# A fused decoder block on one core: the context turned by VectorE from square blocks, the sums behind the first adapter round, one wide rank-4 product

## What is computed

```python
x = x + attention(layernorm(x))            # scores = q k^T / 4, banded by sps_pro, softmax, times v, projection
x = x + gated(layernorm(x), ctx, ctx)      # 8 heads of 32; q k^T times exp(Dtilde - max), over a norm, then group norm
x = x + ffn(layernorm(x))                  # below

# gated: its gates see q, k and v, and k = v = ctx
itilde = einsum('bsd,hd->bhs', concat([q, ctx, ctx]), Wi_w) + Wi_b
ftilde = einsum('bsd,hd->bhs', concat([q, ctx, ctx]), Wf_w) + Wf_b
csum = cumsum(log_sigmoid(ftilde))

# ffn: tokens 1 to 16 of each sequence make low-rank adapters m1 (H x D) and m2 (D x H)
m1 = (even[:, :4, :, None] * odd[:, :4, None, :]).reshape(B, H, D)
m2 = (even[:, 4:, :, None] * odd[:, 4:, None, :]).reshape(B, D, H)
h = gelu(x W1^T + scale * x m1^T + b1)
out = h W2^T + scale * h m2^T + b2
```

## Time and profile before

| | us |
|---|---|
| median of the runs | 2023.12 |
| profiled execution, its own time | 2027.77 |
| its span, first to last instruction | 2026.0 |
| TensorE busy | 1940.2 (96%) |
| VectorE busy | 1522.6 (75%) |
| ScalarE busy | 1125.0 (56%) |
| GpSimd busy | 314.9 (16%) |

### The profile page before, as it was taken

The page is one execution under the profiler, slowest core; times in us unless marked ns, Lnnn a source line. Parts: engine busy times, 40 slices in busy tenths (PEclk is TensorE's granted clock), DMA queues, the critical chain, the costliest instruction groups (busy, mean ns, idle before and its releaser), DMA issues.

```text
span 2026.0 us, 47964 instructions
## 1 busy us (share of the span) xinstructions
PE 1940.2 (96%) x16404; PEld 1464.9 (72%) x16404; DVE 1522.6 (75%) x4318; ACT 1125.0 (56%) x2504; POOL 314.9 (16%) x257
## 2 busy tenths in 40 slices
PE   5789999999999999999999999999999999999988
PEld 4467777777777777777777777777777777777766
DVE  6577787778787778777778778777878777877742
ACT  2455566655556655556655556665555665555551
POOL 1111011111011111111111101111101111111110
PEclk9699999999999999999999999999999999999999
DMA  3000001110001111010110000011000111100000
GB/s 103 22 23 14 30 22 32 32 32 31 12 22 32 32 32 32 11 32 22 32 32 32 17 27 22 32 32 32 32 12 22 32 32 32 32 11 33 13 13 22
DMA packets 65583, 56.43 MB, mean 28 GB/s; under 512 B 13185, under 2 KB 65026, under 8 KB 65554
## 3 DMA queue, kind: packets, MB, share of 16 engines
q1 hardware_dynamic: 65554, 56.05, 8.9%
HBM read 37.15 MB, written 16.78 MB: 27 GB/s over the span
## 4 chain that ended last, share of the span: by engine, by line
PE 93%; DVE 4%; ACT 2%; issue 0%; DMA 0%; SPq 0%; DVEq 0%; ACTq 0%
PE UA L1290 16%; PE UB L1290 5%; PE TB L1232 5%; PE UB L1232 5%; PE UA L1232 5%; PE PV L1232 4%; PE UA L1240 3%; PE TA L1257 3%; PE TB L1372 3%; PE GT L1302 3%; PE TA L1372 3%; PE TA L1197 3%; PE TA L1101 3%; PE TB L1101 3%; PE QQ L1086 2%; PE UA L1310 2%
## 5 line engine op out<-in xcount | busy, mean ns | idle before, releaser
L1290 PE MATMUL UA<-W2f,hs_all 128*128 128x256 f32 x1536 | 349.1, 380 | 2.9 <-DVE ot L943 2.2
L1290 PEld LDWEIGHTS UA<-W2f,hs_all 128*128 128x128 f32 x1536 | 286.5, 190 | 62.3 <-issue 13.9
L957 DVE TENSOR_TENSOR C<-qT,QKs 128x512 f32<-128x512 f32 x256 | 169.3, 690 | 172.3 <-ACT qT L668 153.4
L550 POOL TENSOR_TENSOR Ng<-HT,gnw_b 128x256 f32<-128x256 f32 x128 | 94.9, 741 | 820.4 <-ACT HT L681 820.4
L531 POOL TENSOR_TENSOR xg<-x,gnb_b 128x1024 f32<-128x1024 f32 x32 | 75.9, 2372 | 811.1 <-DVE csum L893 811.1
L1290 PE MATMUL UB<-W2f,hs_all 128*128 128x256 f32 x512 | 115.8, 379 | 0.0
L659 ACT ACTIVATE hs_all<-UA,b1c 128x512 f32<-128x512 f32 x64 | 44.0, 687 | 109.6 <-PE TB L1240 109.6
L1290 PEld LDWEIGHTS UB<-W2f,hs_all 128*128 128x128 f32 x512 | 94.9, 190 | 11.7
L649 ACT ACTIVATE QKs<-TA 128x512 f32<-128x512 f32 x64 | 38.4, 600 | 108.9 <-PE DD L1257 108.9
L1257 PEld LDWEIGHTS TA<-xn2T,ctxT 32*128 32x128 f32 x512 | 63.2, 190 | 30.1 <-issue 27.7
L898 DVE TENSOR_SCALAR band_a<-sc 128x512 f32<-128x512 f32 x32 | 76.7, 2397 | 10.0 <-ACT sc L633 10.0
(11 more groups left out here) (311 smaller groups left out, 5532.3 us busy)
## 6 DMA issues: line engine op xcount, KB each, us to landing
xin<-x SPq DMA_DIRECT2D x32, 512.0 KB, 3.5
ctxn<-ctx SPq DMA_DIRECT2D x32, 512.0 KB, 3.8
out<-ot SPq DMA_DIRECT2D x32, 512.0 KB, 3.0
Ev<-xn SPq DMA_DIRECT2D x512, 1.0 KB
hs_all<-L_ffn_W SPq DMA_DIRECT2D x4, 512.0 KB, 8.7
T<-tok SPq DMA_DIRECT2D x128, 2.0 KB
moving<-parts SPq DMA_DIRECT2D x96, 8.0 KB, 1.9
QKs<-L_attn_W_qkv SPq DMA_DIRECT2D x1, 768.0 KB
```

What stands on the lines that cost most here:

```text
L550: pool.tensor_tensor(Ng[:, b, :].rearrange("p (k n) -> p k n", k=2), HT[:, b % 2, :, 0:P], gnw_b[:, :].rearrange("p (k n) -> p k n", k=2), ...
L957: dve.tensor_tensor(C[:, b % 2, 4 * hf:4 * hf + 4, :].rearrange("p h i -> p (h i)"), dx[hf], QKs[:, b, 4 * hf:4 * hf + 4, :].rearrange("p ...
L1290: ins = pe.matmul(OB[b][:, 0:D], hs_all[:, k, b * S:(b + 1) * S], W2f[:, k, :], start=(i == 0), stop=(i == KH - 1))
```

## The change

Three edits in each step.

1. The context is loaded twice. `ctxn` stays for `vc`. Beside it SyncE issues eight transfers, one for each 32 features, which put the context into `bands` (the two band buffers, now one tensor of 128 x 2 x 512) so that every 32 x 32 square lies where its turned copy is wanted. They wait for `y_ok` and come after the `Ev` rows and before the E rows. VectorE turns all squares in one instruction, behind `head_sums(1)` and ahead of `rinv`. `turn_ctx` and `evac_ctxT` are gone.
2. `sums` moves from behind `up(2)` to behind `up_adapter(0)`. GpSimd's `xg` waits for `xn3l` in place of `csum`.
3. `low_rank` makes all four sequences' products against all tokens in eight matmuls of 512 columns; `gT` adds the bias row and multiplies by `own_g`, which holds the scale for a token's own sequence and zero for the others.

```diff
+        bands = sb("bands", [P, 2, N])
+        band_a, band_b = (bands[:, i, :] for i in range(2))
+        ctx_blocks = bands[:, :, :].rearrange("p k (n c) -> p k n c", c=32)
...
+        c_blocks = ctx_in.rearrange("(g b) (i a) d -> g a (b i) d", b=G, a=32)
...
                 if SELF.on(it):
-                    sp.wait_ge(ctxT_mm.h, ctxT_mm.at(it, 0))
                     sp.wait_ge(vc_ok.h, vc_ok.at(it, 1))
                     sp.dma_start(ctxn[:, :, :], c_g[it]).then_inc(ctx_loaded.h, 16)
...
                 if FFN.on(it):
                     ev_rows(it)
+                if SELF.on(it):
+                    sp.wait_ge(y_ok.h, y_ok.at(it, 1))
+                    for h in range(HEADS):
+                        sp.dma_start(ctx_blocks[32 * (h % 4):32 * (h % 4) + 32, h // 4, :, :],
+                                     c_blocks[it][:, :, 32 * h:32 * h + 32]).then_inc(blocks_loaded.h, 16)
                 if CROSS.on(it):
                     e_rows(it)
...
-                    pool.wait_ge(csum_ok.h, csum_ok.at(it, 1))
+                    pool.wait_ge(xn3l_ok.h, xn3l_ok.at(it, 2))
                     pool.tensor_tensor(xg[:, :, :], x2[:, :, :], gnb_b[:, :].unsqueeze(1).broadcast_to([P, G, D]),
                                        ALU.add).then_inc(xg_ok.h, 1)
...
-            def evac_ctxT(it):
-                evac(it, ctxT_mm, ctxT_ok, [QQ, DD], ctxT, [qk_mm])
...
-                    dve.tensor_scalar(gT[:, :], GT[:, :], sc_b[:, 0:1], bias_row[:, 0:1], ALU.mult, ALU.add)\
-                       .then_inc(gT_ok.h, 1)
+                    dve.scalar_tensor_tensor(gT[:, :].rearrange("p (b s) -> p b s", b=G),
+                                             GT[:, :].rearrange("p (b s) -> p b s", b=G), bias_row[:, 0:1],
+                                             own_g[:, :].unsqueeze(2).broadcast_to([P, G, S]),
+                                             ALU.add, ALU.mult).then_inc(gT_ok.h, 1)
...
                 if cross:
                     head_sums(1)
                 if own:
+                    dve.wait_ge(blocks_loaded.h, blocks_loaded.at(it, HEADS * 16))
+                    dve.wait_ge(qk_mm.h, qk_mm.at(it, 2))
+                    dve.transpose(ctxT[:, :, :].rearrange("p k n -> p (k n)"),
+                                  bands[:, :, :].rearrange("p k n -> p (k n)")).then_inc(ctxT_ok.h, 1)
                     dve.wait_ge(probs_ok.h, probs_ok.at(it, 1))
                     link(dve.reciprocal(rinv[:, :], psums[:, :]))
...
-                    transposes(it, xn3, [QQ, DD], xn3T_mm, [(xn_ok[2], 0)])
+                    transposes(it, xn3, [QQ, DD], xn3T_mm, [(xn_ok[2], 0), (dexp_ok, 0)])
...
-                    elif i == 2 and cross:
-                        sums()
                 if ffn:
                     up_adapter(0)
+                if cross:
+                    sums()
...
-                    for b in range(G):
-                        tok_b = slice(b * S, (b + 1) * S)
-                        for k in range(KD):
-                            for c in range(CB):
-                                ins = pe.matmul(GT[32 * c:32 * c + 32, tok_b], Zo[:, k, 32 * b:32 * b + 32],
-                                                hs_all[:, KD * c + k, tok_b], start=(k == 0), stop=(k == 1))
+                    for k in range(KD):
+                        for c in range(CB):
+                            ins = pe.matmul(GT[32 * c:32 * c + 32, :], Zo[:, k, :], hs_all[:, KD * c + k, :],
+                                            start=(k == 0), stop=(k == 1))
...
-                if own:
-                    turn_ctx(it)
```

More of the change, by code:

```diff
@@ L172, in build @@
         W2f = sb("W2f", [P, KH, D])
+        own_g = sb("own_g", [P, G])
+        sel_g = sb("sel_g", [P, G, CB * R])
         bias_row = sb("bias_row", [P, 1])
@@ L190, in build @@
         sc = sb("sc", [P, N])
-        band_a = sb("band_a", [P, N])
-        band_b = sb("band_b", [P, N])
+        bands = sb("bands", [P, 2, N])
+        band_a, band_b = (bands[:, i, :] for i in range(2))
+        ctx_blocks = bands[:, :, :].rearrange("p k (n c) -> p k n c", c=32)
         y = sb("y", [P, N])
@@ L240, in build @@
         tok = sb("tok", [P, S])
-        Zo = sb("Zo", [P, KD, 40 * G])
+        Zo = sb("Zo", [P, KD, 32])
         E = sb("E", [P, 2, P])
@@ L305, in build @@
         ctx_loaded = per_step("ctx_loaded", SELF, 16)
+        blocks_loaded = per_step("blocks_loaded", SELF, HEADS * 16)
         e_loaded = per_step("e_loaded", CROSS, 16)
@@ L312, in build @@
         xn1T_mm = per_step("xn1T_mm", COMING, 2)
-        ctxT_mm = per_step("ctxT_mm", SELF, 2)
         xn2T_mm = per_step("xn2T_mm", CROSS, 2)
@@ L334, in build @@
         xn1T_ok = per_step("xn1T_ok", COMING, 2)
-        ctxT_ok = per_step("ctxT_ok", SELF, 2)
+        ctxT_ok = per_step("ctxT_ok", SELF, 1)
         xn2T_ok = per_step("xn2T_ok", CROSS, 2)
@@ L514, in _ @@
             pool.memset(lntau[:, :], LN_TAU)
-            pool.memset(bias_row[:, :], 0.0).then_inc(s_idz, 1)
+            pool.memset(bias_row[:, :], 0.0)
+            pool.memset(sel_g[:, :, :], 0.0).then_inc(s_idz, 1)
             pool.wait_ge(s_idz, 3)
@@ L518, in _ @@
                                base=-BIAS_ROW, pattern=[[-1, 1]], channel_multiplier=1)
+            v = sel_g[:, :, :].rearrange("p b (c r) -> p b c r", c=CB)
+            pool.affine_select(out=v, in_=v, compare_op=ALU.not_equal, fill=1.0, base=0,
+                               pattern=[[-8, G], [-32, CB], [-1, R]], channel_multiplier=1)
             for t in (WgT, Z, Zo, E, T, Ev, em):
@@ L746, in step @@
                     evac_xn1T(it)
-                if own:
-                    evac_ctxT(it)
                 if cross:
@@ L838, in _ @@
             dve.wait_ge(s_zero, 1)
+            done(dve.tensor_reduce(own_g[:, :], sel_g[:, :, :], AX_X, ALU.add))
+            done(dve.tensor_scalar(own_g[:, :], own_g[:, :], sc_b[:, 0:1], bias_row[:, 0:1], ALU.mult, ALU.add))
             dve.wait_ge(s_gbias, 16 * (2 * G + 1))
@@ L1094, in turn_xn2 @@
                 transposes(it, xn2, [QQ, DD], xn2T_mm, [(xn_ok[1], 0), (xn3h_ok, 2)])
-            def turn_ctx(it):
-                transposes(it, ctxn, [QQ, DD], ctxT_mm, [(ctx_loaded, 16), (dexp_ok, 2 * G), (c_ok, 2 * G)])
             def project_q(it, m, k):
@@ L1451 @@
 V_BIAS = V_WT + 2 + 2 + 2 + 4
-SETUP_V = V_BIAS + 1 + 2 + 1 + 8 + 1
+SETUP_V = V_BIAS + 2 + 1 + 2 + 1 + 8 + 1
 def kernel(**inputs):
```

## The result

The changed kernel takes 1966.7 us (median of four runs, 1965.5 to 1969.6) against 2022.9 us for the kernel before, measured beside it. The ratio is 0.9725, with a 95% interval from 0.9708 to 0.9741: 56 us or 2.8% faster. The forecast was 1965 us, 58 us less. The profiled execution took 1969.6 us, its span is 1967.8 us, 58.2 us under the span before.

The account below looks back on a forecast made before the run. TensorE, busy 96% of the span, was taken to bound the kernel; savings of 28.2 + 29.5 + 1 us, less 0.5 us for set-up, made 58 us off the 2023.1 us median: 1965 us, range 1955 to 1993 us.

Parts of the forecast that it names:

- The bound: Loop step: the chain stays on TensorE, except 0.68 us on ScalarE's gelu behind the first adapter round.
- the sum: Whole kernel: 28.2 + 29.5 + 1 us saved, less 0.5 us for set-up instructions, about 58 us.
- Transposes: Context transposes leave TensorE's chain: 0.88 us in each of 32 steps, 28.2 us saved.
- The slack of `xn2`: VectorE's `xn2` ahead of its reader: slack shrinks from 3.2 to 2.3 us and holds.
- `sums`: Moved behind the adapter round, it fills the gelu wait and shortens `up(3)`: 0.95 us in 31 steps, 29.5 us.
- Its cover: VectorE and GpSimd timing for moved `sums`: `csum` ready with 0.85 us slack, `acs` with about 0.5 us.
- The wide product: Rank-4 product in `low_rank`: 0.03 us saved a step, 1 us in all; bounds 0 and 0.2 us a step.
- The transfers: SyncE's eight block transfers: 5.1 us at 20 ns a piece, landing 1.5 us before VectorE's turn.
- The slower rival: VectorE waits for blocks if a 128-byte piece costs over 34 ns; 2154 us at 50 ns; chance 0.08.
- The turn: VectorE's one instruction over 1024 columns ahead of `rinv`: 1.23 us, upper bound 2.3 us.
- The slack of the last `C`: VectorE's second `C`, behind the turn, ends 0.52 us later, still 0.3 us before its reader: the thinnest cover.
- the second rival: Last `C` becomes late, TensorE waits 0.8 us a step: 1990 us, range 1975 to 1992; chance 0.22.

Follow-up runs that it names:

- the two experiments on GpSimd's place: Changed kernel with `xg` waiting for `csum` again: 1977.6 us; changed kernel with `sums` back behind `up(2)` and `xg` still early: 2064.5 us.
- the two experiments that used it up: Changed kernel with VectorE's turn done twice: 2009.7 us; changed kernel with half a turn more (512 columns into a spare tile): 1978.7 us.
- the narrow product: Changed kernel with the rank-4 product in 32 matmuls of 128 columns again: 1966.3 us.

## Why the prediction was right

- *The bound.* The chain ran through TensorE for 93% and does so for 94%. The median step fell by 1.82 us; the sum had 0.88 + 0.95 + 0.03 = 1.86, and undoing the parts one by one gives 0.86 + 0.95 + 0.00 = 1.81. Over the whole kernel it had 58 us, and 58.2 were measured in the span, 56 in the medians. That the span agrees to 0.2 us is in part luck: the profiled kernel before lost 1.5 us to a lower clock in one step, and the runs of the changed kernel spread over 4 us.
- *Transposes.* 0.88 us a step forecast, 0.86 by undoing that part. I had counted 32 such steps; in the last of the 30, where TensorE waits for VectorE behind them, the transposes cost nothing, so there it is one fewer. The slack of `xn2` held; nothing else came late.
- *`sums`.* 0.95 forecast, 0.95 measured, with both terms visible: the wait of 0.76 us filled, `up(3)` at 1.40.
- *Its cover.* `csum` was to be ready 0.85 us before `sums`; it ends at 1009.24 and `sums` starts at 1010.04, 0.80. The bands were forecast 4.0 us behind the end of `up(2)`, and end 3.9 us behind it. That GpSimd and VectorE hold each other was read from equal end times; the two experiments on GpSimd's place show how much hangs on it.
- *The wide product.* 1 us forecast, nothing measurable, inside the bounds given.
- *The transfers.* Forecast to be issued within 5.1 us and to have 1.5 us to spare; it was 4.1 and 2.7. I had taken 20 ns for a piece. The busy time of one is 12.6 ns, and the issue was the limit, at 0.53 us from one transfer to the next. The slower rival needed 34 ns and was far off. They move 95 GB/s, where `xin` moves 512 KB in some 1.6 us, and that costs nothing as long as they land in time. By the minimum of 512 bytes in the Trainium skill (DMA: Bandwidth & Descriptors, Specifications) they should be below line rate, and the trace agrees: 12.6 ns for 128 bytes are 10 bytes a ns on one DMA engine, where 50 ns for 1 KB are 20. Whether reading, modifying and writing is a part of the 12.6 ns, no run shows.
- *The turn.* 1.23 us forecast from a two-input pass of the same length, 1.23 measured. The estimate of 2.5 us from the Trainium skill's table (VectorE: DVE Perf Modes, The three transpose paths) would have been double; this case's 0.69 us for 512 and 1.23 for 1024 columns make 1.05 ns a column and 0.15 us for the instruction at any length. At 128 columns that is an estimate of 0.29 us, of which the fixed part is half, so eight such instructions count it eight times.
- *The slack of the last `C`.* 0.3 us forecast, 0.34 and 0.35 by the two experiments that used it up. What I hadn't seen is that the second rival is worse than summed: from a delay somewhere between 0.62 and 1.16 us on, GpSimd's `Ng` adds 0.54 us. At a turn of 2.3 us I had put 0.8 us of waiting a step; by the runs' figures my estimate is now 1.07 + 0.54 - 0.35 = 1.26, which would be 2005 us rather than 1990 and outside my range. No run has a turn of that length.

The first 125 us, before all stages are filled, differ between the profiled executions of all these kernels: the gram product of the first full step starts at 120.4 us with the narrow product and at 127.6 in the kernel before, and in each the granted clock is at its lower level of 1.2 GHz for some 31 to 44 us of that stretch, in which TensorE often waits. These microseconds come and go with the run, so the step is the better yardstick for differences under 5 us.

## What to carry over

When one engine's list is the chain, count an edit by what it takes out of that list, and look for a wait in the list that a movable piece can fill: the largest single gain here was three small products put into 0.76 us of idle time, with 0.2 us saved beside it, because `up(3)` no longer follows another kind of product. Then check each cover by time and not by busy share: which GpSimd instruction runs at the same time as one of VectorE, which of the two starts first, and how long after one engine's end the other starts. A pair of edits can be good together and a loss apart, so undo them one by one and in both orders.

## What the runs showed of the hardware that I had not expected

- A VectorE instruction that is 0.6 us late costs 0.3 us, one that is 1.2 us late costs 1.3: the hold by GpSimd turns a small delay into a large one, by order of start. The one that starts second waits for the end of the other (`C` pair 1.29 or 1.83 us, `Ng` 0.73 or 1.09 us).
- A wait of 1.69 us on TensorE in each step, beside one of 0.76, can cost more than itself: in eight of 30 steps the granted clock fell to its lower level for 3.4 us behind it, 1.53 us more each. In the changed kernel, whose TensorE hardly waits in the loop, the first 29 of the 30 steps all take 58.30 us and none shows it. With 1.35 us of waiting a step (the turn done twice) only the first of the 30 does.
- Thirty-two partitions by sixteen 128-byte pieces, 512 pieces, are issued as fast as the four pieces of 256 bytes of an `Ev` transfer: 4.08 us for eight against 8.80 us for sixteen. The number of transfers costs time on SyncE's queue, the number of pieces in them didn't.
- VectorE's turn of 32 x 32 squares in float32 runs like a plain pass, 1.23 us for 1024 columns and 0.69 us for 512, so 1.05 ns for a column more; two in a row follow each other after 1.16 us.
